# Three pairs of PSUM banks shared in turn by scan drives, projections and turned products, with the fills, sums and early loads reordered to fit

## The chip, the cores and the metric

The kernel runs on one core of one Trainium2 chip. The metric is the device time of one launch in microseconds (us). A row of the trace gives the start of a group of instructions, its length, engine, source line and shapes; PE is TensorE, DVE is VectorE, ACT is ScalarE, POOL is GpSimd, SP is the engine that issues most of the DMAs.

## What is computed

The reference is a two-layer image block over 8 images of 64x64 pixels and 96 channels. The layer that matters here is a selective scan over 4096 time steps, 4 directions, 192 channels and 16 states:

```python
dts, Bs, Cs = jnp.split(x_dbl, [DT_RANK, DT_RANK + D_STATE], axis=2)
delta = jax.nn.softplus(dts + dt_projs_bias[None, :, :, None])
def step(hst, inp):
    u_t, d_t, B_t, C_t = inp
    hst = hst * jnp.exp(d_t[..., None] * A) + (d_t * u_t)[..., None] * B_t[:, :, None, :]
    return (hst, jnp.einsum('bkdn,bkn->bkd', hst, C_t))
```

Before it stand a group normalization, a projection and a 3x3 depthwise convolution with SiLU; behind it a normalization, a gate, an output projection, linear attention over tokens and a feed-forward net in rounded low precision.

## The kernel before, in words

Each engine runs its own hand-written instruction stream, and semaphores tie them together. Per image there are three phases, each closed by a rendezvous of all engines: the scan phase, the merge of the four directions with gate and output projection, and attention with feed-forward (which also makes the next image's convolution).

The scan phase handles one direction after another, each cut into 8 chunks of 512 time steps: 32 chunks per image, 256 in all. A chunk is worked in 12 steps (`NSTEP`). In a step, the 128 partitions hold 32 channels by 4 states, and two states (`a` = 0, 1) lie behind one another in the free dimension. For each step:

- ACT makes the decays, `exp(delta * A)`, twice 512 columns, into the step's own buffer `hst[s]` (`decays`, L671). It runs three steps ahead.
- PE makes the drive, `delta * u * B`, in a pair of PSUM banks (`fill`, L1002): 32 fp32 matmuls, which the trace records as 64 matmuls and 64 weight loads, from turned du against a block pattern of B that a DMA has laid out (`b_diag`).
- DVE does the recurrence in two instructions of 512 columns (L1370), with the decays as factor and the drive from PSUM as addend.
- POOL multiplies the states with C (L484).
- PE sums the 16 states of each channel with `gather` into the two `Y` banks, four steps at a time, in two halves (`sum_states`, L1026): six sums per chunk, called (0,0), (0,1), (1,0), (1,1), (2,0), (2,1) by batch and half. The last two are made during the next chunk. DVE takes the finished sums out of the `Y` banks (`add_sums`), between its two instructions of step 5 of the next chunk.

While a chunk is scanned, the next one (`nx` in the code) is prepared: PE projects u twice, each with a low part (L959) and a high part (L964), for the two halves of delta; ACT copies B and C out of the first projection (`copy_bc`, L624) and applies softplus to both (L615); PE turns B (L975), ACT saves it (L631) and SP writes it to DRAM and reads it back as the block pattern (L375, L382); POOL multiplies delta with u (`times_u`, L469), PE turns the product (`turn_du`, L984), ACT saves it (L639); SP and ACT spread delta by DMA to all partitions (L399, L648), and SP loads C (L390).

PSUM has eight banks of 512 fp32 columns. Before the change, banks 0 to 3 hold two pairs for the drives, so that the fill of step s+2 waits for the scan of step s; 4 and 5 are the `Y` banks; 6 and 7 serve first the projections and then the turned product of the next chunk. The order in which PE works is written out by hand in `body` of its block; `SUM_SLOTS` says at which step a sum stands, steps from 12 on meaning the next chunk.

## Time and profile before

| | us |
|---|---|
| median of 3 runs | 11323.54 (11293.52 to 11373.81) |
| profiled execution, its own time | 11306.72 |
| its span, first to last instruction | 11304.9 |
| PE busy | 9638.9 (85%) |
| DVE busy | 8620.7 (76%) |
| POOL busy | 7841.6 (69%) |
| ACT busy | 6486.2 (57%) |
| mean granted TensorE clock | 0.927 of full |

The time of the profiled execution is 1.8 us more than its span, and lies within the range of the three runs. Busy shares are means over phases with quite different limits; the eight scan phases take about 1070 us each, about 76% of the span.

### The profile page before, as it was taken

To read this page: it belongs to the slowest core of one execution; us is meant where nothing else is said; L and a number is where in the kernel's file an instruction comes from. 1 tells how busy PE (TensorE), PEld (TensorE's weight loads), DVE (VectorE), ACT (ScalarE), POOL (GpSimd) and SP (SyncE) were. 2 spreads that over 40 slices of the span, in tenths; PEclk is the share of its full clock that TensorE was granted. 3 is DMA by queue.
4 is the path that set the end of the run, shared out by engine and by line. 5 is a ranking of instruction groups with operands and counts; after the bars stand their busy time and mean duration, and the time that the engine had idled before them with its cause. 6 is when DMAs were issued, how large, how long until landed. Compare 5 with 4: busy or idle time off the path is not lost.

```text
span 11304.9 us, 500467 instructions
## 1 busy us (share of the span) xinstructions
PE 9638.9 (85%) x224288; PEld 4968.1 (44%) x224288; DVE 8620.7 (76%) x8404; ACT 6486.2 (57%) x9893; POOL 7841.6 (69%) x4027
## 2 busy tenths in 40 slices
PE   7888888888888888888888888898888888888886
PEld 3444344443444434444344443444434444344443
DVE  4898668986589856899568895698956888478884
ACT  4666556665566645666456664566645666456664
POOL 3888538885488854888458884588845888458883
PEclk9999899998999989999889998899989999899997
DMA  3555225552255523555135551355513555145550
GB/s 90 148 147 147 64 77 143 149 141 62 81 142 153 141 55 84 147 149 152 40 96 144 147 148 38 98 146 148 147 35 110 146 143 145 28 116 149 143 144 22
DMA packets 853330, 1301.52 MB, mean 115 GB/s; under 512 B 517231, under 2 KB 518800, under 8 KB 785148
## 3 DMA queue, kind: packets, MB, share of 16 engines
q1 hardware_dynamic: 752892, 1135.15, 36.1%
q10 hardware_dynamic: 98304, 134.35, 4.5%
q8 instruction: 1776, 29.10, 1.2%
q14 instruction: 358, 2.93, 0.1%
HBM read 832.67 MB, written 33.55 MB: 77 GB/s over the span
## 4 chain that ended last, share of the span: by engine, by line
PE 55%; issue 14%; DVE 11%; POOL 9%; SPq 4%; ACT 3%; DMA 2%; ACTq 2%; POOLq 1%; DVEq 0%
PE ps L1002 22%; PE ps L1026 13%; DVE arena L1370 8%; PE ps L934 5%; PE ps L964 5%; POOL arena L484 5%; PE ps L959 4%; SPq L399 3%; PE ps L975 2%; ACTq L648 2%; ACT arena L671 1%; PE ps L984 1%; POOL arena L501 1%; POOL arena L509 1%; POOL arena L536 1%
## 5 line engine op out<-in xcount | busy, mean ns | idle before, releaser
L1370 DVE TENSOR_TENSOR_SCAN arena<-arena,ps 128x512 f32<-128x512 f32 x6144 | 7259.5, 1251 | 899.9 <-PE ps L1002 887.2
L484 POOL TENSOR_TENSOR arena<-arena 128x1024 f32<-128x1024 f32 x3072 | 6613.4, 2185 | 1414.1 <-DMA arena<-c_rows 979.4
L671 ACT ACTIVATE arena<-arena,negA 128x512 f32<-128x512 f32 x6144 | 3952.1, 714 | 1755.5 <-DMA arena<-arena 831.6
L1002 PE MATMUL ps<-arena 64*32 64x128 f32 x196608 | 3966.2, 284 | 1046.9 <-issue 479.5
L1002 PEld LDWEIGHTS ps<-arena 64*32 64x32 f32 x196608 | 2965.3, 107 | 3024.5 <-issue 2997.1
L1026 PE MATMUL ps<-arena,gather 128*32 128x512 f32 x12288 | 2207.4, 631 | 66.9 <-POOL arena L484 50.4
L934 PE MATMUL ps<-arena,wconv 96*64 96x512 f32 (+1 forms) x2304 | 835.9, 629 | 23.7 <-issue 23.7
L469 POOL TENSOR_TENSOR arena<-arena,u_hi 128x512 f32<-128x512 f32 x256 | 327.8, 1280 | 696.1 <-ACT arena L615 696.1
L1026 PEld LDWEIGHTS ps<-arena,gather 128*32 128x32 f32 x12288 | 374.4, 111 | 992.5 <-issue 808.8
L964 PE MATMUL ps<-u_hi,xw_hi 128*128 128x512 f32 x1024 | 671.0, 742 | 3.0 <-issue 3.0
L671 ACT ACT_TABLE_LOAD x256 | 328.4, 1283 | 557.9 <-issue 557.7
L959 PE MATMUL ps<-u_lo,xw_lo 128*128 128x512 f32 x1024 | 589.6, 660 | 55.2 <-SPq L164 47.2
L615 ACT ACTIVATE arena<-ps,dtb 128x512 f32<-128x512 f32 x512 | 341.8, 688 | 341.8 <-PE ps L964 338.2
L934 PEld LDWEIGHTS ps<-arena,wconv 96*64 96x64 f32 (+1 forms) x2304 | 301.9, 172 | 415.4 <-issue 407.9
L469 POOL TENSOR_TENSOR arena<-arena,u_lo 128x512 f32<-128x512 f32 x256 | 328.9, 1285 | 115.8 <-PE ps L984 101.9
L515 POOL TENSOR_TENSOR arena<-arena,power 128x4 f32<-128x4 f32 x64 | 64.8, 1013 | 425.7 <-DVE arena L1401 425.7
L639 ACT ACTIVATE arena<-ps 128x256 f32<-128x256 f32 (+1 forms) x512 | 247.0, 484 | 175.0 <-PE ps L984 174.4
L975 PE MATMUL ps<-ident,arena 16*64 16x16 f32 x4096 | 297.1, 209 | 48.3 <-issue 39.1
L615 ACT ACT_TABLE_LOAD x256 | 328.4, 1283 | 4.7
L984 PE MATMUL ps<-ident,arena 64*128 64x64 f32 (+1 forms) x2048 | 290.4, 264 | 41.5 <-POOL arena L469 34.0
L531 POOL TENSOR_TENSOR arena<-arena 128x1056 f32<-128x1056 f32 x16 | 64.4, 4024 | 372.0 <-DVE arena L1430 372.0
L975 PEld LDWEIGHTS ps<-ident,arena 16*64 16x64 f32 x4096 | 270.7, 138 | 115.2 <-issue 115.2
(155 smaller groups left out, 5648.4 us busy)
## 6 DMA issues: line engine op xcount, KB each, us to landing
arena<-b_runs SPq DMA_DIRECT2D x512, 1024.0 KB, 7.0
arena<-arena SPq DMA_DIRECT2D x4096, 64.0 KB
arena<-c_rows SPq DMA_DIRECT2D x2048, 128.0 KB, 3.8
arena<-arena ACTq DMA_DIRECT2D x2048, 64.0 KB
arena<-in_x SPq DMA_DIRECT2D x128, 192.0 KB, 2.7
out_tokens<-arena SPq DMA_DIRECT2D x64, 192.0 KB, 2.4
c_rows<-arena SPq DMA_DIRECT2D x256, 32.0 KB
b_runs<-arena SPq DMA_DIRECT2D x512, 16.0 KB
```

The source lines that it names most:

```text
L469: pool.tensor_tensor(du.rearrange("p (k h t) -> p h k t", h=2, k=NB), in_time(t_l[v]), in_time(u_lo[:, ch.dir, cols] if v else u_hi[:, col ...
L484: pool.tensor_tensor(ch.weighed(s)[:, :, flip], ch.span(s)[:, :, flip], c_row[:, :, flip], ALU.mult).then_inc(weighted, 1)
L615: act.activation(t_l[v], bank(HI_BANK + v), ACT.Softplus, bias=dtb[:, 1 - v, ch.k:ch.k + 1]).then_inc(delta_done, 1)
L671: act.activation(ch.span(s, a), delta_rep[:, g, :], ACT.Exp, scale=negA[:, ch.k, i:i + 1]).then_inc(decay_ready, 1)
L934: return pe.matmul(to.rearrange("p (r w) -> p r w", w=W), wconv[:, t, channels], xT_img[:, r0:r0 + ROWS, dx:dx + W], start=(t == 0), stop= ...
L959: pe.matmul(bank(HI_BANK + v), xw_lo[:, ch.k, z * P:(z + 1) * P], u_lo[:, ch.dir, bass.ds(ch.t0, T)], start=True, stop=False)
L964: pe.matmul(bank(HI_BANK + v), xw_hi[:, ch.k, z * P:(z + 1) * P], u_hi[:, bass.ds(ch.t0, T)], start=False, stop=True).then_inc(pre_filled, 1)
L975: mm = pe.matmul(to, bc_raw[r, steps(h, k)], ident[r, ch.d0:ch.d0 + NS].rearrange("p (q n) -> p q n", n=RUN), start=True, stop=True)
L984: mm = pe.transpose(bank(HI_BANK + v)[:, k * w:(k + 1) * w], du[r, k * P:(k + 1) * P], ident[r, r])
L1002: mm = pe.matmul(to, du_t[ch.par][rows, k, g * CW:(g + 1) * CW], spots[rows, j, :, :], start=True, stop=True)
L1026: mm = pe.matmul(bank(bk)[row:row + CW, :], gather[:, :], ch.weighed(s, a), start=(s < NG and a == 0), stop=(s >= NG and a == 1))
L1370: dve.tensor_tensor_scan(ch.span(s, a)[:, flip], ch.span(s, a)[:, flip], drive(s % 2)[:, :, a][:, flip], before, ALU.mult, ALU.add).then_i ...
```

## The change

- Banks 0 to 5 become three pairs (`PAIRS`), used in turn. Per chunk the ring takes 14 turns: 12 drives, one for the projections of the next chunk (between the drives of steps 2 and 3) and one for its turned product (between steps 9 and 10). `FREED_BY` names, for each step, the scan that frees its pair. The `Y` banks become 6 and 7.
- PE's order in `body` is new: fills stand up to three steps ahead, both projections stand at steps 0 and 1, both turnings of du at step 7, and the sums at steps 6, 8, 9, 11 and, in the next chunk, 3 and 4.
- The fill of step 5 waits for both softplus and the copy of B and C of the next chunk, since they leave the pair that it takes.
- du has a buffer for each half; POOL makes both halves after steps 2 and 3. ACT applies softplus at step 3 and saves both turned halves at step 9.
- At the start of an image ACT saves the turned B ahead of softplus. At the end of the scan phase SP loads x ahead of the rendezvous, once the decays have been made.

The diff, cut to what matters:

```diff
-        du, bc_raw = cv(T), cv(T)
+        du = [cv(T) for _ in range(2)]
+        bc_raw = cv(T)
...
-        Y_BANK, HI_BANK, LO_BANK = 4, 6, 7
-        SUM_SLOTS = {5: (0, 0), 7: (0, 1), 10: (1, 0), 11: (1, 1), NSTEP + 1: (2, 0), NSTEP + 3: (2, 1)}
+        Y_BANK, PAIRS = 6, 3
+        SUM_SLOTS = {6: (0, 0), 8: (0, 1), 9: (1, 0), 11: (1, 1), NSTEP + 3: (2, 0), NSTEP + 4: (2, 1)}
...
+                self.turn = (kk * NCH + c) * (NSTEP + 2)
+                self.made_in = 0 if first else (self.turn - 9) % PAIRS
+                self.turned_in = 1 if first else (self.turn - 1) % PAIRS
+
+            def drive_in(self, s):
+
+                return (self.turn + 2 + s + (s > 2) + (s > 9)) % PAIRS
...
+                wait_apart(sp, decay_ready, (b + 1) * (K * NCH * NCOL))
+                load_x(sp, b)
                 rendezvous(sp, b, 1)
 
-                load_x(sp, b)
                 wait_apart(sp, x_loaded, (b * 2 + 2) * (16 * NCH))
...
                         if nx:
-                            if s == 4:
+                            if s == 2:
                                 times_u(nx, 0)
-                            if s == 6:
+                            if s == 3:
                                 times_u(nx, 1)
...
                 def pre(ch, nx):
                     copy_bc(ch)
+                    save_bt(ch)
                     softplus(ch, 0)
                     softplus(ch, 1)
+                    save_du(ch, 0)
                     load_delta(ch, 4)
                     load_delta(ch, 5)
-                    save_bt(ch)
-                    save_du(ch, 0)
                     save_du(ch, 1)
...
                             if s == 9:
                                 save_du(nx, 0)
-                            if s == 10:
                                 save_du(nx, 1)
...
+                        if nx and s == 3:
+                            softplus(nx, 0)
+                            softplus(nx, 1)
                         if nx and s == 4:
                             save_bt(nx)
-                            softplus(nx, 0)
-                            softplus(nx, 1)
                             load_delta(nx, 4)
...
                 def project_lo(ch, v):
 
                     z = 1 - v
-                    if not ch.first:
-                        pe.wait_ge(dut_saved, ch.n(2, v - 1))
+                    if v == 0 and not ch.first:
+                        pe.wait_ge(scan_done, ch.n(NSCAN, 2 - NSCAN))
...
                 def turn_du(ch, v):
 
+                    if v == 0 and not ch.first:
+                        wait_apart(pe, scan_done, ch.n(NSCAN, 2 * 7 + 2 - NSCAN))
...
-                def fill(ch, s):
+                FREED_BY = {1: -2, 2: -1, 3: 1, 4: 2, 6: 3, 7: 4, 8: 5, 9: 6, 10: 8, 11: 9}
+
+                def fill(ch, s, nx=None):
 
                     pr, g = s // NG, GROUPS[s]
-                    if s in (0, 2):
-                        wait_apart(pe, dut_saved, ch.n(2, 1 + s // 2))
+                    if s == 0:
+                        wait_apart(pe, dut_saved, ch.n(2, 1 if ch.first else 2))
                     if s % NG == 0:
                         wait_apart(pe, b_loaded[pr], ch.n(16, 16))
-                    if not (ch.first and s < 2):
-                        wait_apart(pe, scan_done, ch.n(NSCAN, 2 * (s - 2) + 2))
+                    if ch.first and s == 1:
+                        wait_apart(pe, delta_done, ch.n(2, 2))
+                        wait_apart(pe, bc_copied, ch.n(1, 1))
+                    elif ch.first and s == 2:
+                        wait_apart(pe, dut_saved, ch.n(2, 2))
+                    elif s == 5:
+                        if nx:
+                            wait_apart(pe, delta_done, nx.n(2, 2))
+                            wait_apart(pe, bc_copied, nx.n(1, 1))
+                    elif s > 0:
+                        wait_apart(pe, scan_done, ch.n(NSCAN, 2 * FREED_BY[s] + 2))
+                    pair = ch.drive_in(s)
...
                     for s in range(NSTEP):
-                        if s + 2 < NSTEP:
+                        if s == 0 and nx:
+                            project_lo(nx, 0)
+                            project_hi(nx, 0)
+                        if s in (1, 2):
                             fill(ch, s + 2)
-                        elif nx:
-                            fill(nx, s + 2 - NSTEP)
...
+                        if s == 1 and nx:
+                            project_lo(nx, 1)
+                            project_hi(nx, 1)
+                        if s == 2 and nx:
+                            turn_b(nx)
+                        if s == 3:
+                            fill(ch, 5, nx)
+                        if 3 <= s < 7:
+                            fill(ch, s + 3)
+                        if s == 7 and nx:
+                            turn_du(nx, 0)
+                            turn_du(nx, 1)
+                        if s in (8, 9):
+                            fill(ch, s + 2)
+                        if s == 10 and nx:
+                            fill(nx, 0)
+                            fill(nx, 1)
+                        if s == 11 and nx:
+                            fill(nx, 2)
```

How PE's stream reads now, in the first half of a chunk. The rows run from the fill of step 2 to sum (2,1) of the chunk before, which DVE awaits inside step 5; the rest of each group's matmuls (rows that end in x31, x7 or x3) is left out. In the kernel before, L1002 is a fill, L1026 a sum, L959 and L964 the parts of a projection, L975 the turning of B:

```order
L959 MATMUL ps<-u_lo,xw_lo 128x512 [waits dut_saved]
L1002 MATMUL ps<-arena 32x128 [waits dut_saved,scan_done]
L964 MATMUL ps<-u_hi,xw_hi 128x512
L1002 MATMUL ps<-arena 32x128 [waits scan_done]
L1026 MATMUL ps<-arena,gather 32x512 [waits weighted]
L1002 MATMUL ps<-arena 32x128 [waits scan_done]
L975 MATMUL ps<-ident,arena 64x2x8 [waits bc_copied,bt_saved]
L1002 MATMUL ps<-arena 32x128 [waits scan_done]
L964 MATMUL ps<-u_hi,xw_hi 128x512
L1026 MATMUL ps<-arena,gather 32x512 [waits weighted]
```

In the changed kernel L1026 is a fill, L1049 a sum, L969 and L974 the parts of a projection, L985 the turning of B; the rows begin behind the fill of step 2 and sum (1,1):

```order
L969 MATMUL ps<-u_lo,xw_lo 128x512 [waits scan_done]
L974 MATMUL ps<-u_hi,xw_hi 128x512
L1026 MATMUL ps<-arena 32x128 [waits scan_done]
L969 MATMUL ps<-u_lo,xw_lo 128x512
L974 MATMUL ps<-u_hi,xw_hi 128x512
L1026 MATMUL ps<-arena 32x128 [waits scan_done]
L985 MATMUL ps<-ident,arena 64x2x8 [waits bc_copied,bt_saved]
L1026 MATMUL ps<-arena 32x128 [waits delta_done,bc_copied]
L1026 MATMUL ps<-arena 32x128 [waits b_loaded1,scan_done]
L1049 MATMUL ps<-arena,gather 32x512 [waits weighted]
L1026 MATMUL ps<-arena 32x128 [waits scan_done]
L1049 MATMUL ps<-arena,gather 32x512 [waits weighted]
```

Sum (2,1) stood behind the fill of step 5 and now stands behind those of 6 and 7; all four parts of the projections are ahead of it; the fills of steps 5 and 6 touch.

PE's stream in the second half. Before, from the fill of step 7 (the first one behind sum (2,1) and the fill of step 6); L984 is a turning of du:

```order
L1002 MATMUL ps<-arena 32x128 [waits scan_done]
L1026 MATMUL ps<-arena,gather 32x512 [waits weighted,y_saved]
L1002 MATMUL ps<-arena 32x128 [waits scan_done]
L984 MATMUL ps<-ident,arena 128x64 [waits du_done]
L1002 MATMUL ps<-arena 32x128 [waits scan_done]
L1026 MATMUL ps<-arena,gather 32x512 [waits weighted]
L1002 MATMUL ps<-arena 32x128 [waits scan_done]
L984 MATMUL ps<-ident,arena 128x128 [waits du_done]
L1002 MATMUL ps<-arena 32x128 [waits scan_done]
```

Changed, from the fill of step 8 (the first one behind sum (2,1)); L996 is a turning of du. The fill that waits for dut_saved and b_loaded0 is that of step 0 of the next chunk:

```order
L1026 MATMUL ps<-arena 32x128 [waits scan_done]
L1026 MATMUL ps<-arena 32x128 [waits scan_done]
L1049 MATMUL ps<-arena,gather 32x512 [waits weighted,y_saved]
L996 MATMUL ps<-ident,arena 128x64 [waits scan_done,du_done]
L996 MATMUL ps<-ident,arena 128x128 [waits du_done]
L1026 MATMUL ps<-arena 32x128 [waits scan_done]
L1049 MATMUL ps<-arena,gather 32x512 [waits weighted]
L1026 MATMUL ps<-arena 32x128 [waits scan_done]
L1049 MATMUL ps<-arena,gather 32x512 [waits weighted]
L1026 MATMUL ps<-arena 32x128 [waits dut_saved,b_loaded0]
L1026 MATMUL ps<-arena 32x128 [waits scan_done]
L1026 MATMUL ps<-arena 32x128 [waits scan_done]
```

The fills of steps 8 and 9 (waiting for scans 5 and 6) follow each other with nothing between; the fills of steps 0, 1 and 2 of the next chunk follow each other too.

ACT's stream about softplus. Before (L671 a decay, L631 the saving of turned B, L615 softplus, L648 the spreading of delta by DMA):

```order
L671 ACTIVATE arena<-arena,negA 128x512 [waits delta_loaded1,summed]
L671 ACTIVATE arena<-arena,negA 128x512 [waits summed]
L671 ACTIVATE arena<-arena,negA 128x512 [waits summed]
L631 ACTIVATE arena<-ps 64x128 [waits b_written,b_turned]
L615 ACT_TABLE_LOAD [waits delta_loaded2,du_done]
L615 ACTIVATE arena<-ps,dtb 128x512 [waits pre_filled]
L615 ACTIVATE arena<-ps,dtb 128x512 [waits delta_loaded0,delta_loaded1,du_done,pre_filled]
L648 DMA arena<-arena 32x512 [waits decay_ready,delta_done]
```

Changed (L681, L641, L625, L658 in the same roles):

```order
L681 ACTIVATE arena<-arena,negA 128x512 [waits delta_loaded1,summed]
L681 ACTIVATE arena<-arena,negA 128x512 [waits summed]
L625 ACT_TABLE_LOAD [waits delta_loaded2,du_done]
L625 ACTIVATE arena<-ps,dtb 128x512 [waits pre_filled]
L625 ACTIVATE arena<-ps,dtb 128x512 [waits delta_loaded0,delta_loaded1,du_done,pre_filled]
L681 ACT_TABLE_LOAD
L681 ACTIVATE arena<-arena,negA 128x512 [waits summed]
L641 ACTIVATE arena<-ps 64x128 [waits b_written,b_turned]
```

Softplus comes one step earlier, behind the decays of step 6 in place of step 7.

## Rows read from the trace of the kernel before

**Rows 1.** Eight scan phases: length, busy time per engine, granted clock, DMA share, GB/s
```profile
183.60:1255.00 1071.40, 941.39 (x27024) 510.96 (x27008) 947.96 (x830) 660.83 (x1012) 895.74 (x443) 0.96 0.52 144
...
sum 8575.60, PE 7518.38 PEld 4082.01 DVE 7576.90 ACT 5287.90 POOL 7182.65; mean PE 939.80 PEld 510.25 DVE 947.11 ACT 660.99 POOL 897.83
```

**Rows 2.** Who waited for whom, whole run: us in total, times, longest
```profile
DVE arena L1370 <- PE ps L1002: 887.2, 620, 28.5
...
PE ps L1002 <- issue: 479.5, 382, 4.6
PE ps L1002 <- DVE arena L1370: 410.9, 362, 2.6
```

**Rows 3.** Timeline of PE through one chunk: start, us, instructions [idle before]
```profile
864.12 1.27 PE L1002 MATMUL ps<-arena 64*32 64x128 f32 x64
867.13 1.18 PE L1002 MATMUL ps<-arena 64*32 64x128 f32 x64 [1.74 <-DVE arena L1370]
868.24 1.91 PE L1026 MATMUL ps<-arena,gather 128*32 128x512 f32 x8
870.08 1.20 PE L1002 MATMUL ps<-arena 64*32 64x128 f32 x64
871.21 0.46 PE L984 MATMUL ps<-ident,arena 64*128 64x64 f32 x4
871.81 1.18 PE L1002 MATMUL ps<-arena 64*32 64x128 f32 x64
...
883.29 1.13 PE L959 MATMUL ps<-u_lo,xw_lo 128*128 128x512 f32 x2
884.35 1.21 PE L1002 MATMUL ps<-arena 64*32 64x128 f32 x64
...
888.60 1.07 PE L1026 MATMUL ps<-arena,gather 128*32 128x512 f32 x8
...
890.71 1.10 PE L975 MATMUL ps<-ident,arena 16*64 16x16 f32 x16
891.74 0.88 PE L1002 MATMUL ps<-arena 64*32 64x128 f32 x37
894.60 0.78 PE L1002 MATMUL ps<-arena 64*32 64x128 f32 x27 [1.98 <-issue]
895.31 2.07 PE L964 MATMUL ps<-u_hi,xw_hi 128*128 128x512 f32 x2
897.32 1.60 PE L1026 MATMUL ps<-arena,gather 128*32 128x512 f32 x8
```

**Rows 4.** Timeline of DVE in the same chunk
```profile
864.26 0.69 DVE L1352 COPY u_lo<-ps 128x512 f32<-128x512 f32 x1 [2.55 <-PE ps L1026]
...
865.70 22.37 DVE L1370 TENSOR_TENSOR_SCAN arena<-arena,ps 128x512 f32<-128x512 f32 x19
...
899.00 0.69 DVE L1352 COPY u_lo<-ps 128x512 f32<-128x512 f32 x1 [2.29 <-PE ps L1026]
```

**Rows 5.** Page, costliest groups: softplus and its table load on ACT
```profile
L615 ACT ACTIVATE arena<-ps,dtb 128x512 f32<-128x512 f32 x512 | 341.8, 688 | 341.8 <-PE ps L964 338.2
...
L615 ACT ACT_TABLE_LOAD x256 | 328.4, 1283 | 4.7
```

**Rows 6.** Timeline at the start of the second image's scan phase
```profile
1558.53 1.07 PE L975 MATMUL ps<-ident,arena 16*64 16x16 f32 x16 [0.77 <-ACT arena L624]
...
1566.70 0.27 ACT L631 ACTIVATE arena<-ps 64x128 f32<-64x128 f32 x1 [4.46 <-issue]
...
1577.63 3.65 PE L1002 MATMUL ps<-arena 64*32 64x128 f32 x128 [12.83 <-DMA arena<-b_runs]
```

**Rows 7.** Timeline at the end of the first image's scan phase
```profile
1237.02 5.02 ACT L671 ACTIVATE arena<-arena,negA 128x512 f32<-128x512 f32 x8 [0.63 <-PE ps L1026]
...
1267.30 4.80 SPq L354 DMA_DIRECT2D arena<-in_x  x8
...
1275.26 1.92 PE L1074 MATMUL ps<-ident,arena 128*96 128x128 f32 x8 [9.59 <-DMA arena<-in_x]
```

More of the change, by code:

```diff
@@ L103, in build @@
         gsm = sb("gsm", [D, 8])
-        ARENA = 25568
+        ARENA = 25920
         arena = sb("arena", [P, ARENA])
@@ L464, in times_u @@
                     pool.wait_ge(delta_done, ch.n(2, v + 1))
-                    if not (ch.first and v == 0):
-                        pool.wait_ge(du_turned, ch.n(2, v))
+                    if not ch.first:
+                        pool.wait_ge(du_turned, ch.n(2, 0))
                     cols = bass.ds(ch.t0, T)
                     in_time = lambda ap: ap.rearrange("p (h k t) -> p h k t", h=2, k=NB)
-                    pool.tensor_tensor(du.rearrange("p (k h t) -> p h k t", h=2, k=NB), in_time(t_l[v]),
+                    pool.tensor_tensor(du[v].rearrange("p (k h t) -> p h k t", h=2, k=NB), in_time(t_l[v]),
                                        in_time(u_lo[:, ch.dir, cols] if v else u_hi[:, cols]), ALU.mult).then_inc(du_done, 1)
@@ L614, in softplus @@
                             act.wait_ge(delta_loaded[i], ch.n(32 * NJ, 0))
-                    act.activation(t_l[v], bank(HI_BANK + v), ACT.Softplus, bias=dtb[:, 1 - v, ch.k:ch.k + 1]).then_inc(delta_done, 1)
+                    act.activation(t_l[v], bank(2 * ch.made_in + v), ACT.Softplus, bias=dtb[:, 1 - v, ch.k:ch.k + 1]).then_inc(delta_done, 1)
                 def copy_bc(ch):
@@ L623, in copy_bc @@
                     r = slice(ch.d0, ch.d0 + 2 * NS)
-                    act.activation(bc_raw[r, :], bank(HI_BANK)[r, :], ACT.Copy).then_inc(bc_copied, 1)
+                    act.activation(bc_raw[r, :], bank(2 * ch.made_in)[r, :], ACT.Copy).then_inc(bc_copied, 1)
                 def save_bt(ch):
@@ L638, in save_du @@
                     w, d = ((DHI, slice(DLO, DI)), (DLO, slice(0, DLO)))[v]
-                    act.activation(du_t[ch.par][:, :, d], bank(HI_BANK + v)[:, 0:NB * w].rearrange("p (k d) -> p k d", d=w), ACT.Copy).then_inc(dut_saved, 1)
+                    act.activation(du_t[ch.par][:, :, d], bank(2 * ch.turned_in + v)[:, 0:NB * w].rearrange("p (k d) -> p k d", d=w), ACT.Copy).then_inc(dut_saved, 1)
                 def load_delta(ch, g):
@@ L1000, in fill @@
                                 rows = slice(h * TB, (h + 1) * TB)
-                                to = ps[j * CW:(j + 1) * CW, 2 * (s % 2) + h, k * 2 * TB:(k + 1) * 2 * TB].rearrange("p (t a) -> p t a", a=2)
+                                to = ps[j * CW:(j + 1) * CW, 2 * pair + h, k * 2 * TB:(k + 1) * 2 * TB].rearrange("p (t a) -> p t a", a=2)
                                 mm = pe.matmul(to, du_t[ch.par][rows, k, g * CW:(g + 1) * CW], spots[rows, j, :, :], start=True, stop=True)
@@ L1014, in pre @@
                     fill(ch, 1)
-                    project_lo(nx, 0)
-                    project_lo(nx, 1)
+                    fill(ch, 2)
                 def sum_states(ch, batch, a):
@@ L1057, in body @@
                             sum_states(before, *SUM_SLOTS[s + NSTEP])
-                        if s == NSTEP - 1 and then:
-                            project_lo(then, 1)
                     if nx is None:
@@ L1369, in body @@
                             before = Chunk(ch.b, ch.kk, ch.c - 1).final(s, a) if kind else 0.0
-                            dve.tensor_tensor_scan(ch.span(s, a)[:, flip], ch.span(s, a)[:, flip], drive(s % 2)[:, :, a][:, flip],
+                            dve.tensor_tensor_scan(ch.span(s, a)[:, flip], ch.span(s, a)[:, flip], drive(ch.drive_in(s))[:, :, a][:, flip],
                                                    before, ALU.mult, ALU.add).then_inc(scan_done, 1)
```

19 lines of the change are left out of this document (3 added, 16 removed).

## Prediction

> **What bounds the kernel now.** I read the scan phases first, since they are three quarters of the span. The view by stretches [rows 1] gives 8575.6 us for eight phases of 32 chunks, so 33.5 us per chunk. DVE is busy 947 us of a mean 1072, PE 940, POOL 898, ACT 661: two engines near their limit and none at it. The reader should see that busy shares alone don't decide this; who waits for whom does. The waits [rows 2] show DVE held up by fills for 887.2 us, and PE held up by scans for only 410.9 us, 1.6 us per chunk, with another 479.5 us "issue" inside the fills.
>
> So I followed PE through one chunk [rows 3]. From the fill of step 7 at 867.13 to the end of sum (2,1) at 898.92 there is no wait for another engine in 31.8 us. Then DVE takes the sums: in the same chunk one round earlier, it starts add_sums at 864.26, right behind sum (2,1), and the second half of scan 5 at 865.70 [rows 4]; PE, which has the fill of step 6 to do meanwhile (864.12), then waits 1.74 us and starts the fill of step 7 at 867.13. The distance from the end of sum (2,1) to that fill is thus 3.0 us, and the loop "PE's work, add_sums, half a scan, PE's work" is what sets the period. At 899.00 the next round begins.
>
> What a chunk costs PE, from starts that follow each other without a wait [rows 3]: a fill 1.11, a sum of batch 0 1.84, a part of a projection 1.06, the turning of B 1.03, a turning of du 0.60. A sum of batch 1 or 2 is 1.07 long and, with the same overlap of 0.07 that fills show, costs 1.00. Twelve fills, two and four sums, four parts, one turning of B and two of du make 13.3 + 3.7 + 4.0 + 4.2 + 1.0 + 1.2 = 27.4 us. The loop holds all of it but the fill of step 6: 26.3 + 3.0 = 29.3. The measured 33.5 leaves 4.2 us per chunk of extra. Of these, 1.9 are the "issue" gaps (479.5 over 256 chunks), as at 894.60, where a fill stops for 1.98 us in its middle; about 1.1 are stretches at the lower of the two granted clocks (mean 0.96 in the phases, so about 4% of 27.4), as in the part at 895.31 that takes 2.07 in place of 1.13; the last 1.2 I can't assign.
>
> **The change, part by part.** *PE's order around the add.* The instructions are the same in number. What changes is where PE stops. After sum (2,1) DVE again needs add_sums and the second half of scan 5, 3.0 us. But PE has nothing to do in them: the next fill is that of step 8, and it waits for scan 5 (FREED_BY 8: 5). Behind it stands the fill of step 9, which waits for scan 6, and behind step 9's fill, sum (0,0) and both turnings of du the fill of step 10, which waits for scan 8. A scan of one step is twice 1.17 us (22.37 us for 19 halves, less the tail [rows 4]), 2.34. So from the end of sum (2,1) to the start of the fill of step 10 there are 3.0 + 3 x 2.34 + 0.1 = 10.1 us, of which PE uses 5.3. From there to the next sum (2,1) PE has ten fills (10, 11, then 0 to 7), five sums, four projection parts and the turning of B without any wait that could bind: 11.1 + 1.84 + 4.0 + 4.2 + 1.0 = 22.2. The new loop is 32.3 us against 29.3: the two fills that now stand ahead of the sums DVE waits for, and the stretch of 7 us in which DVE sets the pace, are its price. The scans of steps 9 to 11 and of the next 0 to 5 run beside PE and are not on it; the third pair of banks helps DVE there, where it is early anyway and then waits for the sums.
>
> *Extra.* PE's stalls come with its work. In proportion, 4.2 x 22.2 / 26.3 = 3.5 us; the bounds are 0 and 4.2. That gives 35.8. In the stretch where DVE sets the pace, fill, sum and turnings take 4.15 beside two scans of 4.68; a stall over 0.5 there shows, 0.2 on average. Then fills touch that had something between them: 0, 1, 2 and 5, 6. A fill is 128 recorded instructions in 1.11 us, and the mean stall is 479.5 / 382 = 1.26 us [rows 2]. Three new pairs would cost from 0 to 3.8 us; I take 0.4, near the lower end, because rows 2 show only 1.5 stalls per chunk of twelve fills. The period becomes 36.4 us.
>
> The Trainium skill has a rule that speaks against counting these gaps. In "Runtime: NRT & Kernel Launch", section "Instruction fetch mechanics", PE's instruction store is given as 128 KiB, a FIFO refilled in blocks of 256 instructions, with the crossing of a block mostly hidden. By that rule the gaps would not be lack of instructions; the 479.5 us of "issue" in rows 2, in the middle of fills, speak against it here. What a refill in pauses would give is a rival below.
>
> *Softplus ahead of fill 5.* That fill now waits for ACT. After the first projection, ACT has a copy (at most 0.7, by the length of a softplus), four decays at 0.63 (eight in 5.02 [rows 7]), the table load 1.28 and two softplus at 0.69 [rows 5]: 5.9 us. PE has a fill, two parts, a fill and the turning of B in between, 5.4 plus 0.8 of extra. I count 0; the bounds are 0 and 0.5. ACT and POOL, at 20.7 and 28.1 us per chunk [rows 1], stay under the period. The second du buffer lets POOL go without waiting for PE; POOL isn't on the loop, so 0.
>
> *Which chunks.* An image's first chunk has no sums from before it, and its last prepares nothing; I count 30 of 32, 240 in all: 240 x (36.4 - 33.5) = +696 us.
>
> *x ahead of the rendezvous.* x is loaded at 1267.30 and PE first uses it at 1275.26 [rows 7]. Its cover is the end of the last chunk: the decays are done at 1242.04, 25 us ahead. What is late next is the rendezvous itself, so 7.9 us go per image, 63 in all; bounds 0 and 66.
>
> *Turned B early.* ACT saves turned B at 1566.70, though PE has turned it by 1559.60; the first fill, at 1577.63, waits for the block pattern that comes of it [rows 6]. Saving it right behind the turning gives 7.0 us, 56 in all. Late next are the first decays, which wait for delta's DMAs; these are issued about where they were, and I take them to be just in time. Bounds 20 and 58. I take 121 us for both loads.
>
> *Sum.* On the profiled execution: 11306.7 + 696 - 121 = 11882. The median of the runs is 17 us above that execution, half of which I add: 11890 us. A measurement of this kernel can tell about 1% from no change.
>
> **The rivals.** *The pauses refill the instruction store (same).* PE now stands for 4.8 us per chunk around fills 8 to 10. If the supply of instructions catches up there, the 1.9 us of "issue" fall away: 32.3 + 1.6 + 0.2 = 34.1, and 240 x 0.6 - 121 = +23, so 11330. For it: the gaps carry no other engine's name. Against it: PE waits 1.74 us per chunk today and still stalls later, in the fill of step 5. (The store that the Trainium skill gives in "Runtime: NRT & Kernel Launch", section "Instruction fetch mechanics", 2048 instructions for PE, would make this the outcome.)
>
> *The loop is DVE's and not PE's (faster).* If the stalls of DVE on fills were what the ring cures, 887.2 us less up to 28.5 (the longest [rows 2]) at each of eight starts, about 660, would go, at the place where a fill now comes late behind scan 4 or 5: 11307 - 660 - 121 = 10526 at the best, and 10900 if the nominal loop of 32.3 held without any extra. It decides once PE's extra is under 1.5 us per chunk. Against it: PE's stretch of 31.8 us without a wait.
>
> *The order changes nothing (slightly faster).* If the pause around the add stayed at 1.74 us, because PE could catch up between fills 8 and 10, only the two loads would count: 11307 - 121 = 11186. Against it: both fills wait for scans that start only behind the add.
>
> *Dense fills starve (slower still).* At one full stall of 1.26 us for each chunk on top, the period is 37.7, +1008 - 121: 12200.
>
> **How the numbers follow.** The loop on PE, with the dense case in it, 0.79; refill 0.10; nothing but the loads 0.06; the ring's full gain 0.05. The likeliest gives 11890. The range must reach from inside the refill case to the dense case: 11350 to 12200, leaving out 0.11 for the two faster rivals, some 0.04 of the refill and 0.04 above. Slower by over 1% (above 11437) 0.81, within 1% 0.09, faster 0.10.
>
> **What would show it.** In the profile after: the scan phases' mean from 1072 to about 1160 us; DVE's wait for add_sums (today 2.29 in [rows 4]) at 4 us or more in each chunk, and its waits for fills shorter; PE's wait for scans from 410.9 to about 1100 us, most of it ahead of fills 8, 9 and 10; no wait on x at the start of the merge; the first fill of an image 11 us behind the turned B in place of 18 (1577.63 against 1559.60 [rows 6]). It is wrong if PE shows no pause ahead of fill 8, if DVE reaches add_sums together with sum (2,1), or if the "issue" gaps fall under 200 us.

## The result, and the profile after

The changed kernel takes 11900.41 us (median of 4 runs, 11880.88 to 11908.14), the kernel before 11308.53 in the same comparison (4 runs, 11270.81 to 11373.81): a ratio of 1.0527, with an interval of 1.0494 to 1.0559. It is 5% slower; the forecast was 11890. The profiled execution took 11903.69, 597 us more than the one before.

The scan phases first. This is the view by stretches of the kernel after, one stretch per phase; the first phase and the sum, in the columns of [rows 1].

```profile
179.32:1346.43 1167.11, 958.04 (x26990) 541.38 (x26975) 950.39 (x830) 665.04 (x1015) 904.15 (x445) 0.91 0.48 134
...
sum 9304.06, PE 7642.62 PEld 4331.36 DVE 7606.27 ACT 5319.52 POOL 7233.37; mean PE 955.33 PEld 541.42 DVE 950.78 ACT 664.94 POOL 904.17
```

The phases take 9304 us in all. For the comparison of single chunks I measure every phase from its first scan to its last, in all kernels; the kernel before then has 8584, so +720. The rest of the span went from 2721 to 2598, -123. DVE, ACT and POOL are as busy as in [rows 1], within 7 us per phase. Their work didn't get longer; they wait more. PE's busy time rose by 15 us a phase while its granted clock fell to 0.91.

The waits of the kernel after (us in total, times, longest), which answer to [rows 2]:

```profile
PE ps L1026 <- DVE arena L1398: 934.0, 555, 3.1
DVE arena L1398 <- PE ps L1026: 750.2, 835, 4.5
PE ps L1026 <- issue: 503.1, 490, 4.5
...
DVE u_lo L1384 <- PE ps L1049: 257.2, 64, 6.2
DVE y_d L1377 <- PE ps L1049: 246.8, 64, 6.5
DVE y_d L1384 <- PE ps L1049: 244.8, 64, 7.2
DVE u_lo L1380 <- PE ps L1049: 232.2, 64, 6.6
...
PE ps L1026 <- ACT arena L625: 142.9, 176, 2.7
```

In this kernel L1026 is the fill, L1049 the sum, L1398 the scan, and L1377 to L1385 are `add_sums`. PE's fills wait for scans for 934 us in place of 411, `add_sums` waits 981 us for the sums (356 in the kernel before, by the same four rows), and the stalls inside fills are hardly changed, 503 in place of 480. A stall, here and below, is idle time of PE in a fill that carries no other engine's name ("issue").

PE through one inner chunk, from the fill of step 7 to the fill of step 8 one round later (the kernel after; columns as in [rows 3]):

```profile
783.24 1.20 PE L1026 MATMUL ps<-arena 64*32 64x128 f32 x64
784.36 1.06 PE L1049 MATMUL ps<-arena,gather 128*32 128x512 f32 x8
788.05 1.18 PE L1026 MATMUL ps<-arena 64*32 64x128 f32 x64 [2.62 <-DVE arena L1398]
790.27 1.96 PE L1026 MATMUL ps<-arena 64*32 64x128 f32 x64 [1.04 <-DVE arena L1398]
792.16 2.52 PE L1049 MATMUL ps<-arena,gather 128*32 128x512 f32 x8
794.61 1.05 PE L996 MATMUL ps<-ident,arena 64*128 64x64 f32 x8
795.59 1.20 PE L1026 MATMUL ps<-arena 64*32 64x128 f32 x64
796.71 1.91 PE L1049 MATMUL ps<-arena,gather 128*32 128x512 f32 x8
...
803.32 1.36 PE L1026 MATMUL ps<-arena 64*32 64x128 f32 x72 [0.59 <-issue]
...
810.09 0.65 PE L1026 MATMUL ps<-arena 64*32 64x128 f32 x21 [1.66 <-issue]
...
819.35 1.07 PE L1049 MATMUL ps<-arena,gather 128*32 128x512 f32 x8
...
823.35 1.41 PE L1026 MATMUL ps<-arena 64*32 64x128 f32 x64 [2.93 <-DVE arena L1398]
```

And DVE beside it, in the kernel after, which answers to [rows 4]:

```profile
779.84 1.22 DVE L1398 TENSOR_TENSOR_SCAN arena<-arena,ps 128x512 f32<-128x512 f32 x1 [3.45 <-PE ps L1026]
785.50 0.69 DVE L1384 TENSOR_TENSOR y_d<-ps,y_d 128x512 f32<-128x512 f32 x1 [4.43 <-PE ps L1049]
786.10 0.67 DVE L1385 TENSOR_TENSOR y_hi<-ps,y_hi 64x512 f32<-64x512 f32 x1
786.70 12.48 DVE L1398 TENSOR_TENSOR_SCAN arena<-arena,ps 128x512 f32<-128x512 f32 x11
```

Sum (2,1) starts at 784.36. Until it is done DVE waits 4.43 us; then DVE adds and scans, and PE waits 2.62 us ahead of the fill of step 8 and 1.04 ahead of that of step 9. The next round's fill of step 8 starts at 823.35, 35.30 us later. The two engines take turns, as forecast. Over all 256 chunks DVE waits 3.83 us on average for the add (981 / 256), a little less than in this one.

The start of the second image's scan phase in the kernel after, which answers to [rows 6]:

```profile
1648.06 1.07 PE L985 MATMUL ps<-ident,arena 16*64 16x16 f32 x16 [0.77 <-ACT arena L634]
...
1649.17 0.27 ACT L641 ACTIVATE arena<-ps 64x128 f32<-64x128 f32 x1 [1.25 <-PE ps L985]
...
1653.47 5.79 ACTq L658 DMA_DIRECT2D arena<-arena  x8
...
1659.31 0.60 ACT L649 ACTIVATE arena<-ps 128x512 f32<-128x512 f32 x1 [5.53 <-issue]
...
1659.45 3.16 PE L1026 MATMUL ps<-arena 64*32 64x128 f32 x99 [4.21 <-DMA arena<-b_runs]
...
1663.45 6.23 ACT L681 ACTIVATE arena<-arena,negA 128x512 f32<-128x512 f32 x10 [2.24 <-DMA arena<-arena]
...
1664.27 7.89 DVE L1398 TENSOR_TENSOR_SCAN arena<-arena,ps 128x512 f32<-128x512 f32 x7 [20.66 <-ACT arena L681]
```

The first fill comes 10.3 us behind the turned B (1659.45 against 1649.13), where it was 18 before. But the first scan no longer waits for it: it waits for the first decays, and these for delta's DMAs, whose eight issues from ACT's own queue (1653.47) hold its next save until 1659.31. From the first projection to the first scan the time fell from 25.3 to 20.4 us, 4.9 of the 7.0 that I counted.

The end of the first phase in the kernel after, which answers to [rows 7]:

```profile
1333.85 4.41 SPq L363 DMA_DIRECT2D arena<-in_x  x8
...
1353.53 1.91 PE L1102 MATMUL ps<-ident,arena 128*96 128x128 f32 x8 [1.80 <-DVEq L164]
```

x is issued 20 us ahead of its use, and the wait on it (9.59 us) is gone; what remains is the rendezvous.

### The profile page after: what moved, and what is told of

The parts are those of the page before. It is cut to its first block, busy times and chain, and to the rows that moved or that the text cites. A ratio compares the mean times of both kernels' runs of the same rounds, so it can differ in the third digit from the quotient of the medians.

```text
span 11901.9 us, 500467 instructions
## 1 busy us (share of the span) xinstructions
PE 9752.2 (82%) x224288; PEld 5219.9 (44%) x224288; DVE 8643.2 (73%) x8404; ACT 6499.6 (55%) x9893; POOL 7880.6 (66%) x4027
## 3 DMA queue, kind: packets, MB, share of 16 engines
q8 instruction: 1776, 29.10, 1.1%
## 4 chain that ended last, share of the span: by engine, by line
PE 57%; issue 15%; DVE 10%; ACT 9%; POOL 5%; SPq 1%; ACTq 1%; DMA 1%; POOLq 1%; DVEq 0%
PE ps L1026 24%; PE ps L1049 17%; DVE arena L1398 7%; PE ps L944 5%; ACT arena L681 5%; PE ps L969 3%; PE ps L974 2%; ACT L625 2%; PE ps L996 2%; POOL arena L494 2%; ACT arena L625 1%; POOL arena L511 1%; SPq L408 1%; POOL arena L519 1%; PE ps L985 1%
## 5 line engine op out<-in xcount | busy, mean ns | idle before, releaser
L1398 DVE TENSOR_TENSOR_SCAN arena<-arena,ps 128x512 f32<-128x512 f32 x6144 | 7279.3, 1251 | 928.7 <-PE ps L1026 750.2
L681 ACT ACTIVATE arena<-arena,negA 128x512 f32<-128x512 f32 x6144 | 3931.7, 712 | 2690.6 <-PE ps L1049 2248.8
L1026 PE MATMUL ps<-arena 64*32 64x128 f32 x196608 | 4065.1, 297 | 1617.5 <-DVE arena L1398 934.0
L1026 PEld LDWEIGHTS ps<-arena 64*32 64x32 f32 x196608 | 3182.6, 112 | 3232.9 <-issue 3201.8
L1049 PE MATMUL ps<-arena,gather 128*32 128x512 f32 x12288 | 2352.3, 652 | 76.2 <-issue 49.1
L1049 PEld LDWEIGHTS ps<-arena,gather 128*32 128x32 f32 x12288 | 392.9, 114 | 932.5 <-issue 872.9
L969 PE MATMUL ps<-u_lo,xw_lo 128*128 128x512 f32 x1024 | 603.7, 672 | 66.9 <-SPq L164 47.1
L974 PE MATMUL ps<-u_hi,xw_hi 128*128 128x512 f32 x1024 | 539.9, 610 | 0.5 <-issue 0.5
L996 PEld LDWEIGHTS ps<-ident,arena 64*128 64x128 f32 (+1 forms) x2048 | 201.3, 147 | 320.6 <-issue 302.9
L625 ACT ACTIVATE arena<-ps,dtb 128x512 f32<-128x512 f32 x512 | 324.6, 683 | 7.5 <-PE ps L974 4.1
L974 PEld LDWEIGHTS ps<-u_hi,xw_hi 128*128 128x128 f32 x1024 | 202.5, 198 | 262.2 <-issue 262.2
L969 PEld LDWEIGHTS ps<-u_lo,xw_lo 128*128 128x128 f32 x1024 | 158.6, 195 | 332.6 <-DVE arena L1398 181.4
```

What stands on the lines that cost most here:

```text
L625: act.activation(t_l[v], bank(2 * ch.made_in + v), ACT.Softplus, bias=dtb[:, 1 - v, ch.k:ch.k + 1]).then_inc(delta_done, 1)
L681: act.activation(ch.span(s, a), delta_rep[:, g, :], ACT.Exp, scale=negA[:, ch.k, i:i + 1]).then_inc(decay_ready, 1)
L969: pe.matmul(bank(2 * ch.made_in + v), xw_lo[:, ch.k, z * P:(z + 1) * P], u_lo[:, ch.dir, bass.ds(ch.t0, T)], start=True, stop=False)
L974: pe.matmul(bank(2 * ch.made_in + v), xw_hi[:, ch.k, z * P:(z + 1) * P], u_hi[:, bass.ds(ch.t0, T)], start=False, stop=True).then_inc(pre_ ...
L996: mm = pe.transpose(bank(2 * ch.turned_in + v)[:, k * w:(k + 1) * w], du[v][r, k * P:(k + 1) * P], ident[r, r])
L1026: mm = pe.matmul(to, du_t[ch.par][rows, k, g * CW:(g + 1) * CW], spots[rows, j, :, :], start=True, stop=True)
```

## The experiments

The loop theory (PE and DVE take turns around `add_sums`) predicts the time of any order of sums and fills; its rivals were stalls from dense fills, the clock, and the early loads. "Period" is the mean distance between the first scans of inner chunks, 30 of each image: 33.58 in the kernel before, 36.59 after. A time in us stands for the median; each ratio is to the kernel before, run beside it.

**The old slots of the sums in the new ring.**

```diff
-        SUM_SLOTS = {6: (0, 0), 8: (0, 1), 9: (1, 0), 11: (1, 1), NSTEP + 3: (2, 0), NSTEP + 4: (2, 1)}
+        SUM_SLOTS = {5: (0, 0), 7: (0, 1), 10: (1, 0), 11: (1, 1), NSTEP + 1: (2, 0), NSTEP + 3: (2, 1)}
```

> The changed kernel with the sums at the steps at which the kernel before has them (5, 7, 10, 11, and 1 and 3 of the next chunk); ring, fills, projections, softplus and early loads stay. Loop theory (PE's work, add_sums, half a scan, PE's work): the fill of step 7 now runs beside the add (pause about 1.9 us), sum (0,0) fills the gap between the fills of steps 8 and 9, sum (0,1) the one ahead of step 10. 27.4 + 1.9 + the 4.1 us of extra that the kernel before had = 33.4 us per chunk, total about 11200 us. Rival (the ring itself is what costs: fills that touch, the fill of step 5 behind softplus, both projections in a row): at least 35.5 us per chunk, over 11600 us. Rival (the clock: the time came with more stretches at the lower granted clock): the clock stays near 0.90 and the period above 35 us.

Measured: 11342.96 (10 runs), ratio 1.0028 (1.0010 to 1.0046), period 34.57. Two of PE's waits in this kernel:

```profile
PE ps L1026 <- issue: 740.9, 724, 3.8
PE ps L1026 <- DVE arena L1398: 492.7, 525, 2.1
```

Moving the sums alone takes back 2.0 of the 3.0 us per chunk, with ring, early fills and everything else in place. The loop theory gave 33.4, so 1.2 us per chunk are missing, and 1.0 of them stands in the first row: the stalls inside fills are 741 us in 724 stalls, against 480 in 382 in the kernel before and 503 in 490 in the changed one. The two rivals fall with this run: the ring alone would have cost at least 35.5 us per chunk, and the clock, at 0.943, is higher than in the kernel before (0.927). In this order the fills of steps 10, 11, 0 and 1 stand in a row.

**The last two sums one step ahead, two variants.** Both put sums (2,0) and (2,1) right behind the fill of step 5 at step 3; the second also puts the sums of batch 0 a step earlier.

```diff
-        SUM_SLOTS = {6: (0, 0), 8: (0, 1), 9: (1, 0), 11: (1, 1), NSTEP + 3: (2, 0), NSTEP + 4: (2, 1)}
+        SUM_SLOTS = {6: (0, 0), 8: (0, 1), 9: (1, 0), 11: (1, 1)}
...
                             fill(ch, 5, nx)
+                            if not ch.first:
+                                sum_states(before, 2, 0)
+                                sum_states(before, 2, 1)
```

> The changed kernel with sums (2,0) and (2,1) moved from behind the fills of steps 6 and 7 to right behind the fill of step 5; nothing else. Loop theory: two fills (2.2 us) run beside add_sums and the half scan, so the pause ahead of the fill of step 8 falls from 3.0 to 0.8 us; the other pauses stay (about 1.2 ahead of the fill of step 9, 0.5 ahead of 10). 27.4 + 2.5 + 4.1 = 34.0 us per chunk, total about 11300 us. Ring rival and clock rival: less than 1 us per chunk gained, over 11650 us.

> As e2_sums_first, and sums (0,0) and (0,1) one step earlier (5 and 7 in place of 6 and 8), so that each stands in a pause: (0,0) between the fills of steps 8 and 9, (0,1) ahead of that of step 10. Loop theory: only the 0.8 us pause is left; 27.4 + 0.8 + 4.1 = 32.3 us per chunk, total about 10900 us, faster than both kernels. Ring rival and clock rival: not under 11500 us. If PE's extra grows as it stands less, 33.3 us per chunk and 11150 us.

Measured: 11223.28 (5 runs), ratio 0.9923 (0.9893 to 0.9953), period 34.17; and 11206.14 (4 runs), 0.9913 (0.9881 to 0.9944), period 33.72. The first came out as the loop theory said, 34.0. The second missed its lower figure, 32.3, and came near the case in which PE's extra grows, 33.3. Its PE waits less for scans (321 us against 443 in the first) and is held by other things: stalls are 558 us (480 in the kernel before), and softplus takes 216 us, 0.8 per chunk, which the theory had left out.

**The add one step later.** The order of PE is untouched; only DVE's `add_sums` goes from the middle of step 5 to that of step 6.

```diff
-                                if s == 5 and a == 1 and not ch.first:
+                                if s == 6 and a == 1 and not ch.first:
```

> The changed kernel with one change on DVE alone: add_sums stands between the halves of step 6 in place of step 5, so that scan 5 no longer waits for sum (2,1), and the fill of step 8 can follow that sum at once. Loop theory: the pause ahead of the fill of step 8 goes (3.0 us), one of 1.9 us comes ahead of that of step 9, the next is 0.5: 27.4 + 2.4 + extra of 4.1 to 4.3 = 34.0 us per chunk, total about 11300 us. Rival (PE's order or the ring costs by itself, whatever DVE waits for): over 11700 us.

Measured: 11322.0 (10 runs), ratio 0.9989 (0.9965 to 1.0012), period 34.15 where 34.0 was forecast. This is the decisive run: not one instruction of PE, ACT or POOL has moved, and 578 us are gone. PE around the fill of step 8 in this kernel:

```profile
637.92 1.20 PE L1026 MATMUL ps<-arena 64*32 64x128 f32 x64
640.67 1.18 PE L1026 MATMUL ps<-arena 64*32 64x128 f32 x64 [1.56 <-DVE arena L1398]
...
645.36 1.22 PE L1026 MATMUL ps<-arena 64*32 64x128 f32 x64 [0.69 <-DVE arena L1398]
```

Scan 5 is now whole before the add, so the fill of step 8 (637.92) follows the sum without a pause, and only the fill of step 9 (640.67) waits, 1.56, and that of step 10, 0.69. The pauses sum to 594 us in place of 934.

**The sums spread between the fills.** The second variant above, with sum (1,1) between the next chunk's fills of steps 0 and 1, so that no three fills touch.

```diff
-        SUM_SLOTS = {5: (0, 0), 7: (0, 1), 9: (1, 0), 11: (1, 1)}
+        SUM_SLOTS = {5: (0, 0), 7: (0, 1), 9: (1, 0)}
...
-                        if s == 10 and nx:
-                            fill(nx, 0)
-                            fill(nx, 1)
+                        if s == 10:
+                            if nx:
+                                fill(nx, 0)
+                            sum_states(ch, 1, 1)
+                            if nx:
+                                fill(nx, 1)
```

> As e3_sums_first_early, and sum (1,1) moved from behind the fill of step 2 of the next chunk to between those of steps 0 and 1, so that these two fills no longer touch. Starvation theory (touching fills run PE out of instructions): the gaps inside the fills of steps 0 to 2 (1.27 us per chunk in e3) fall by about half, period 0.4 to 0.6 us shorter, total 11060 to 11110 us. Rival (instruction supply is a matter of the mean rate, or the loop is elsewhere): no change, 11206 us within 0.3%.

Measured: 11248.68 (10 runs), ratio 0.9925 (0.9900 to 0.9950), period 34.06. My explanation for the stalls fell. Per inner chunk, the stalls in the fill of step 1 went from 0.31 us to 0.04, but those of steps 4 and 8 rose, from 0.23 to 0.41 and from 0.36 to 0.49; in all 2.25 us against 2.18. Spreading moves the stalls and doesn't remove them. (The kernel doubles as a test of the position of sum (1,1), which is worth nothing.)

**PE kept busy in the pause.** One or two groups of idle matmuls, written into columns of a `Y` bank that nothing reads, stand ahead of the fills of steps 8 and 9.

```diff
+                        if s in (5, 6) and nx:
+                            wait_apart(pe, bt_saved, nx.n(1, 1))
+                            for _ in range((2, 1)[s - 5]):
+                                pe.matmul(bank(Y_BANK + 1)[DHI:P, P:T], ident[:, 0:DHI], u_lo[:, 1, 0:T - P], start=True, stop=True)
```

> The changed kernel with idle matmuls in PE's pauses (two of 384 columns ahead of the fill of step 8, one ahead of that of step 9, into an unused corner of a bank; about 2.4 us of work per chunk that nobody reads). If the lower granted clock of the changed kernel (0.896) follows from the pauses (PE idle, then dense), the clock rises to 0.93 or more and the time falls by 100 us or more. If the clock falls with the amount of work, it stays at 0.896 or under and the time is the same or longer, up to +240 us.

Measured: 11782.24 (4 runs), ratio 1.0416 (1.0378 to 1.0455), 118 us less than the changed kernel; mean granted clock 0.947 in place of 0.896; period 36.04. The same view by stretches as above, of this kernel, and PE in its pause:

```profile
179.04:1324.31 1145.27, 973.38 (x27114) 531.72 (x27097) 949.13 (x830) 665.10 (x1015) 903.99 (x445) 0.97 0.49 136
...
sum 9178.54, PE 7798.08 PEld 4286.42 DVE 7590.10 ACT 5320.05 POOL 7230.54; mean PE 974.76 PEld 535.80 DVE 948.76 ACT 665.01 POOL 903.82
```

```profile
738.72 1.50 PE L1075 MATMUL ps<-u_lo,ident 128*64 128x384 f32 x4
741.47 1.49 PE L1026 MATMUL ps<-arena 64*32 64x128 f32 x64 [1.25 <-DVE arena L1402]
742.90 0.86 PE L1075 MATMUL ps<-u_lo,ident 128*64 128x384 f32 x2
```

PE does more and the phases are 126 us shorter, though the stalls inside fills rose from 503 to 592 us. So the pause costs twice: its own length, and, net of these stalls, 0.5 us per chunk in the clock behind it. The same idle group once per chunk in the kernel before, ahead of the fill of step 7, whose pause is 1.74 us [rows 3]:

```diff
+                        if s == 5 and nx:
+                            wait_apart(pe, bt_saved, nx.n(1, 1))
+                            pe.matmul(bank(Y_BANK + 1)[DHI:P, P:T], ident[:, 0:DHI], u_lo[:, 1, 0:T - P], start=True, stop=True)
                         if s + 2 < NSTEP:
                             fill(ch, s + 2)
```

> The kernel before with one idle matmul of 384 columns (0.8 us) ahead of the fill of step 7, where PE waits 1.6 us per chunk for add_sums and the half scan. If the lower granted clock follows from PE's pauses, the mean clock rises from 0.927 to 0.94 or more and the time falls by 30 to 150 us. If the pause here is too short to matter, clock and time stay within 0.5%.

Measured: 11286.73 (10 runs), ratio 0.9987 (0.9966 to 1.0007), clock 0.927 as before. No effect there.

**The early loads by themselves.** Three kernels: both loads early in the kernel before (x ahead of the rendezvous, turned B ahead of softplus); x alone; and the changed kernel with both undone.

```diff
+                wait_apart(sp, decay_ready, (b + 1) * (K * NCH * NCOL))
+                load_x(sp, b)
                 rendezvous(sp, b, 1)
-                load_x(sp, b)
...
                     copy_bc(ch)
+                    save_bt(ch)
                     softplus(ch, 0)
                     softplus(ch, 1)
+                    save_du(ch, 0)
                     load_delta(ch, 4)
                     load_delta(ch, 5)
-                    save_bt(ch)
-                    save_du(ch, 0)
                     save_du(ch, 1)
```

> The kernel before with the two early loads alone: x ahead of the rendezvous, and the turned B saved ahead of softplus at the start of an image, du saved as in the change. Prediction's term: 121 us less, about 11190 us. Rival: hidden anyway or eaten by the rendezvous, less than 30 us.

> The kernel before with x alone loaded ahead of the rendezvous. Prediction's term: 63 us less, about 11255 us. With e4_loads_only at 78 us less, that would leave 15 us for the turned B in place of the 56 predicted (given back in the first chunk). Rival: both give about half, 11280 us.

> The changed kernel with both early loads undone (x behind the rendezvous, turned B saved behind softplus at an image's start), so that PE's new order and the ring stand alone. Prediction's terms: 121 us more than the changed kernel, 12020 us. If only what e4_loads_only and e8_x_only showed in the old order comes back, 80 us more, 11980 us.

Measured: both 11240.34 (4 runs), ratio 0.9925 (0.9905 to 0.9944), -78 us, where -121 was forecast; x alone 11246.55 (10 runs), 0.9932 (0.9904 to 0.9961), -81 us; the changed kernel without them 11973.71 (4 runs), 1.0596 (1.0555 to 1.0638), 73 us above the changed one. The trace splits it, by the mean time from the last scan of an image to the next image's first high projection part, and from there to its first scan:

| kernel | last scan to projection, us | projection to first scan, us |
|---|---|---|
| before | 302.9 | 25.0 |
| before, x early | 292.1 | 23.3 |
| before, both early | 292.8 | 19.9 |
| after | 294.1 | 19.8 |
| after, both late | 300.6 | 24.2 |

In the old order x brings 10.8 us at each of seven such places, 76, which fits its run. Turned B then brings 3.4 per image, 27 in all, but the medians of the two runs (-78 and -81) show none of it: 27 us is 0.24%, less than the width of either interval, so these runs can't tell it from nothing. In the changed kernel x brings 6.5 and turned B 4.4, 46 + 35 = 81, near the 73 of the runs. The order and ring alone come to 11973.71 - 11310.92 (the kernel before in that comparison) = +663 us, where I had counted +696.

**Softplus one step earlier on ACT.** On top of the best order above, since its PE waited 216 us for softplus.

```diff
-                        if nx and s == 3:
+                        if nx and s == 2:
                             softplus(nx, 0)
                             softplus(nx, 1)
```

> e3_sums_first_early with softplus one step earlier on ACT, ahead of the decays of step 6 in place of behind them, so that the fill of step 5 waits less for it. In e3 that wait is 216 us in all, 0.9 us per chunk. If it is on the loop: 100 to 200 us less than e3, 11050 us. Rival (PE only takes the time back in gaps between instructions): within 30 us of e3's 11206 us.

Measured: 11117.81 (4 runs), ratio 0.9839 (0.9792 to 0.9886), period 33.39. It is 88 us below the same kernel without this edit (their intervals just touch) and 1.6% faster than the kernel before: the lowest of all that ran. The wait in that kernel with softplus at step 3, and in this one:

```profile
PE ps L1026 <- ACT arena L625: 216.2, 179, 3.5
```

```profile
PE ps L1026 <- issue: 651.2, 659, 3.7
PE ps L1026 <- DVE arena L1401: 293.5, 476, 2.2
...
PE ps L1026 <- ACT arena L625: 78.7, 74, 2.9
```

138 us of waiting went, while the stalls inside fills rose by 93, from 558 to 651. They are now PE's largest idle time in the list, over twice its waits for scans ahead of fills.

## Why the prediction was right

*The loop.* Right, and shown by the add one step later: the same PE stream with the add at another place is 2.44 us per chunk shorter. Forecast 36.4 us per chunk, measured 36.59 for inner chunks; +696 for the phases, measured +720.

*From the sum (2,1) to the fill of step 10.* I had 10.1 and 0.2 on average; the mean over inner chunks is 11.3. PE waits 2.62 and 1.04 ahead of the fills of steps 8 and 9 (2.83 and 0.78 on average), as forecast, but then nothing holds the fill of step 10, which I had waiting for scan 8: it starts at 795.59 right behind the turnings (0.02 us of wait on average). In this stretch PE and not DVE is late in the end, since sum (0,0) takes longer, 2.86 on average in place of 1.96 (here 2.52, at 792.16). So the size of this term is right within 1.0 us, and its reason is only half right: I priced the work behind the pause at the clock ahead of it.

*From the fill of step 10 to the next sum (2,1).* I had 22.2 plus 3.5 of extra and 0.4 for fills that touch, 26.1; the mean is 25.2. Stalls inside fills grew by 24 us in all (503.1 against 479.5), a tenth of a microsecond per chunk. This term was 0.9 too large, and the two errors nearly cancel: that the total is better than its parts is luck.

*Softplus ahead of the fill of step 5.* Counted 0 with 0.5 as the bound; PE waited 142.9 us in all, 0.56 per chunk. I had compared the two chains at their nominal lengths, without any wait on ACT's side; that this is the reason, no run shows directly. Hardly visible here, it was worth 88 us once the loop was mended.

*The loads.* 121 forecast, -78 and -73 measured. By the trace of the changed kernel x is 46 of my 63 and turned B 35 of my 56. The step that failed is "the first decays just in time": the first scan now starts 5.6 us behind the first fill on average, where it was 2.1, and waits for decays that wait for delta, as the row at 1663.45 shows. So half of the 7.0 is given back at once. For x I named the rendezvous as what is late next, but gave it no time; PE now waits for it (1.80 us at 1353.53). The part of the span outside the scan phases did shrink by 123 us; with the loads undone it is still 37 below the kernel before (2683.8 against 2720.9), so those 37 come with the order and the ring, at the phases' edges, and I can't assign them to one edit.

*The rivals.* That pauses refill the instruction supply is refuted: PE stands over 3 us at the add in each chunk, and the stalls are not fewer. The ring's full gain does not exist as long as DVE waits for the sums; in the orders that mend this, at most 1.6% came of it, the loads and the earlier softplus, where this rival gives 3.6% at least (10900). The ring's own part isn't shown at all: with the best order of sums it stands at 0.9913, and the old kernel with the two loads alone at 0.9925. Only the earlier softplus goes clearly below that, and it was not run in the old order. That nothing but the loads would count is excluded by the 2.62 us at 788.05. Dense fills do starve, but not by touching: in the changed kernel the stalls went from 382 to 490, which is 0.1 us per chunk, not 1.26.

*What would show it.* Mean phase 1160 forecast, 1163 measured. DVE's wait for the add at 4 us or more in each chunk: 4.43 in the chunk shown, but 3.83 on average, and 4 or more in only 35 of 100 chunks, so this sign was set too high. Its waits for fills shorter: 750 us in place of 887. PE's waits for scans 1100: 934. No wait on x: none. First fill 11 us behind the turned B: 10.3.

## What to carry to other kernels

When two engines hand results back and forth, find the place in each period where both directions meet, and count what the first engine does between the last thing the second waits for and the first thing that waits for the second; an add moved by one step was worth almost 5% here with no instruction changed. A deeper ring of buffers bought nothing here while another handover closed the loop, and reordering the producer for the ring can lengthen just that handover. Price the work behind a long pause at the clock that it will get, and test the order in pieces, since a good edit (here the early loads and, later, softplus) can be hidden by a bad one beside it.

## What the runs showed of the hardware

*The clock behind a pause.* In the scan phases of the changed kernel the granted clock is at its lower level (0.5 of the upper) for 1718 us, in the kernel before for 721, and with idle matmuls in the pause for 481. Of the 325 such stretches that begin in the scan phases of the changed kernel, 239 begin between 1 us ahead of the first matmul of step 8's fill and 3.5 us behind it, so at the end of the pause around the add. In the kernel before, 13 of 149 begin there around its fill of step 7, whose pause is 1.74 us [rows 3], and filling that pause changed nothing (0.927 both times). With the long pause filled, 8 of 120 begin there. I had expected the clock lower in proportion to PE's share, not at a place of its own.

PE's work in these stretches is slower. A fill without a stall takes a median of 1.55 us from its first matmul to its last, in place of 0.92. In the changed kernel, from 711.51 to 718.34 the clock is at the lower level, and these are the fill of step 9 and the sum (0,0), which take 1.20 and 1.91 at the upper one (as at 783.24 and 796.71 above):

```profile
712.80 1.96 PE L1026 MATMUL ps<-arena 64*32 64x128 f32 x64 [1.15 <-DVE arena L1398]
714.69 3.63 PE L1049 MATMUL ps<-arena,gather 128*32 128x512 f32 x8
```

Still, filling the pause gained 118 us, far less than the 1240 us of low clock that went. Part of the difference shows in other rows: the stalls inside fills are 89 us more, and PE now waits 0.39 us per chunk for scan 8 ahead of the fill of step 10, in place of 0.02, so DVE sets the pace there again. The rest I can't assign.

*The stalls inside fills.* Two rows of the page of the kernel after, engines with their instruction counts, and the queue that carries instructions:

```profile
PE 9752.2 (82%) x224288; PEld 5219.9 (44%) x224288; DVE 8643.2 (73%) x8404; ACT 6499.6 (55%) x9893; POOL 7880.6 (66%) x4027
...
q8 instruction: 1776, 29.10, 1.1%
```

PE has 448,576 of the 500,467 recorded instructions, and 29.10 MB in 1776 packets is 16 KB each. In the kernels before and after, the stalls inside fills (382 and 490) end about 1.4 us after such a packet has ended (1.24 to 1.58 for nine in ten; of times picked at random, 6 in 100 lie in that band). From the end of that packet to the end of the next the median is 4.2 us before and 4.4 after. The Trainium skill, in "Runtime: NRT & Kernel Launch", section "Instruction fetch mechanics", has instructions come in blocks of 16 KiB, 256 instructions, and calls the crossing mostly hidden. The size of the packets agrees with the trace. Hidden the crossings are not in these fills: 128 instructions are done in 1.11 us, so 256 take 2.2 where the next block takes over 4.

Among the kernels with the ring, the two in which PE waits longest for other engines have the fewest stalls, 503 us (changed) and 471 (add later); the others have 558 to 741. The kernel before doesn't fit in: it waits less than all of them and has 480. That the supply of instructions sets a mean rate fits the kernels with the ring, the run with spread sums and the 93 us more behind the earlier softplus. It was not tested directly (by a fill of fewer instructions, say), so it stays an argument; what is shown is the tie of each stall's end to a packet's.
